# Convolution taps' spectra in four 31-row products on four row groups of PE, in a five-phase audio tower kernel

## The reference

```python
logits = (x @ Wl.T + bl).reshape(B, T, H, K)              # T 125, H 4, K 31
w = softmax(where(valid, logits, -inf), axis=-1)
y = einsum('bthk,btkhd->bthd', w, windows(x)) + bias      # dynamic convolution over time
z = conv1d(y, Wc, 'VALID') + bc                           # Wc (512, 128, 31)
hT = selu(z) @ W2.T + b2
```

## Time and profile before

| what | us |
|---|---|
| median of three executions | 2453.52 |
| lowest, highest | 2449.77, 2454.09 |
| the profiled execution, its own time | 2452.1 |
| its span, first to last instruction | 2450.3 |
| PE busy over the span | 2134.8 (87%) |
| L261, the products of the taps, busy | 134.5, 256 records |

### The profile page before, as it was taken

One profiled execution on the slowest core, in us unless ns is written; L12 is line 12 of the kernel. 1 busy time (PEld: TensorE's weight loads), 2 busy tenths in 40 slices (PEclk: granted clock), 3 DMA queues, 4 the chain that ended last, 5 costly groups with the idle time before them and its releaser, 6 DMA issues. The chain is left out here.

```text
span 2450.3 us, 41718 instructions
## 1 busy us (share of the span) xinstructions
PE 2134.8 (87%) x14183; PEld 1496.8 (61%) x14183; DVE 1588.2 (65%) x3564; ACT 1230.3 (50%) x2063; POOL 915.0 (37%) x763
## 2 busy tenths in 40 slices
PE   5799999979998599999999997999999995776671
PEld 4567868855555466666666664777777774555450
DVE  4432333346777588888888875676767664666673
ACT  2334464344554367677667675555655562332330
POOL 0000000013443378777778772000000001786772
PEclk9999999989999699999999999999999996678995
DMA  7660010019920100000000000000000001214554
GB/s 262 245 245 18 27 34 11 1 43 419 420 117 2 69 1 1 0 0 0 0 0 0 0 1 20 1 0 0 0 0 0 0 1 45 83 43 122 165 154 154
DMA packets 64688, 165.46 MB, mean 68 GB/s; under 512 B 12310, under 2 KB 43460, under 8 KB 55084
## 3 DMA queue, kind: packets, MB, share of 16 engines
q1 hardware_dynamic: 51564, 148.42, 17.0%
q0 software_dynamic: 7104, 12.71, 1.5%
q10 hardware_dynamic: 5888, 2.62, 0.4%
HBM read 68.81 MB, written 96.86 MB: 68 GB/s over the span
## 5 line engine op out<-in xcount | busy, mean ns | idle before, releaser
L1261 POOL TENSOR_TENSOR c_both<-c_hid 128x512 f32<-128x512 f32 x384 | 491.6, 1287 | 144.5 <-ACT c_hid L1234 106.2
L1234 ACT ACTIVATE c_hid<-c_scaled,c_b 128x1024 f32<-128x1024 f32 x384 | 437.1, 1150 | 172.9 <-DVE c_scaled L1308 158.0
L1308 DVE TENSOR_TENSOR c_scaled<-c_p_h,c_shares 128x1024 f32<-128x1024 f32 x384 | 454.5, 1215 | 80.5 <-PE c_p_h L1177 79.5
L1182 PE MATMUL c_p_o<-c_both,c_w 128*128 128x512 f32 x768 | 390.8, 591 | 0.0
L1175 PE MATMUL c_p_h<-c_x_hi,c_w_hi 128*128 128x512 f32 x384 | 291.9, 760 | 2.6 <-DVE c_w_lo L1331 2.6
L624 POOL TENSOR_TENSOR d_ln_rstd<-d_ln_var,d_ln_power 128x2 f32<-128x2 f32 x48 | 33.4, 696 | 525.3 <-DVE d_ln_var L620 525.3
L240 POOL COPY a_work<-a_vec 128x64 f32<-128x64 f32 x4 | 1.2, 303 | 444.4 <-PE a_p_A L322 256.0
L1182 PEld LDWEIGHTS c_p_o<-c_both,c_w 128*128 128x128 f32 x768 | 144.3, 188 | 36.1 <-issue 2.2
L1176 PE MATMUL c_p_h<-c_x_lo,c_w_hi 128*128 128x512 f32 x384 | 152.6, 397 | 0.0
L1492 PEld LDWEIGHTS d_p_s<-d_kk,d_q_bd 128*128 128x128 f32 x768 | 123.9, 192 | 45.9 <-issue 45.9
L1177 PE MATMUL c_p_h<-c_x_hi,c_w_lo 128*128 128x512 f32 x384 | 151.9, 396 | 0.0
(11 more groups left out here) (331 smaller groups left out, 4658.6 us busy)
## 6 DMA issues: line engine op xcount, KB each, us to landing
slots<-b_blank SPq DMA_DIRECT2D x56, 1040.0 KB, 23.7
band_scratch<-a_work SPq DMA_DIRECT2D x16, 1024.0 KB, 5.7
a_work<-band_scratch SPq DMA_DIRECT2D x16, 1023.5 KB, 7.9
e_wb<-e_weights SPq DMA_DIRECT2D x63, 164.0 KB, 2.5
a_raw<-in_Wc SPq DMA_DIRECT2D x16, 512.0 KB, 3.6
e_xb<-slots SPq DMA_DIRECT2D x63, 130.0 KB, 2.2
e_yb<-e_again SPq DMA_DIRECT2D x12, 512.0 KB, 5.6
a_work<-in_x_tok SPq DMA_DIRECT2D x16, 256.0 KB, 8.2
```

What stands on the lines that cost most here:

```text
L1182: nc.tensor.matmul(p_o[s][:, 0:N], w2[:, q, :], both[q % SLOTS][:, :], start=(q == 0), stop=(q == NQ - 1)).then_inc(s_down, 1)
L1234: nc.scalar.activation(hid[q % SLOTS][:, :, :], scaled[q % SLOTS][:, :, :], ACT.Gelu, bias=b1[:, q:q + 1]).then_inc(s_ge, 1)
L1261: nc.gpsimd.tensor_tensor(both[q % SLOTS][:, :], hid[q % SLOTS][:, 0, :], hid[q % SLOTS][:, 1, :], ALU.add).then_inc(s_bo, 1)
L1308: v.tensor_tensor(scaled[q % SLOTS][:, :, :], p_h[q % SLOTS][:, 0:N].unsqueeze(1).to_broadcast([128, 2, N]), shares[s][:, :, :], ALU.mult) ...
```

## The change

`raw` now has 32 rows for a channel slot r (31 taps and an empty one), four slots, so one column block m of raw holds channels 0 + m, 32 + m, 64 + m and 96 + m of a chunk. `dft_k` is the 125-column transform of 31 taps, four times below one another (128 rows, 125 columns). `weights(v)` makes a set: for four m, four products of 31 rows and 125 columns, each on its own row group of PE and into its own bank `p_V[r]`. A set covers 16 channels, four of the old products; there are 32 sets. A bank is copied in one piece (`weights_out(v, r)`), 4 channels x 125, now read at a stride of 125. In the first stage DVE copies all four, two a group; in the turn phases ACT copies r = 0 and 1, DVE r = 2 and 3, one each a group. A set is made in every other (even) group. It waits until all four copies of the set before are done.

The two more banks come from `p_y` and `p_out`, which have one buffer each now, so taps, to_time and project wait for the reader of group k - 1.

```diff
-        dft_k = sb("dft_k", [4 * KT, 4 * NF2])
+        dft_k = sb("dft_k", [128, NF2])
...
-        p_V = [pb("p_V0"), pb("p_V1")]
-        p_y = [pb("p_y0"), pb("p_y1")]
-        p_out1 = pb("p_out1")
-        p_conv, p_out = p_y, [p_log, p_out1]
+        p_V = [pb(f"p_V{r}") for r in range(4)]
+        p_y = pb("p_y")
+        p_conv, p_out = p_y, p_log
...
+        PER, NSET = 4, NO * MPO // 4
+        CHUNK = MPO // PER
+
+        def copied(v):
+
+            late = max(v - CHUNK, 0)
+            return 2 * late, 4 * min(v, CHUNK) + 2 * late
...
-            def weights(m):
-
-                if m % MPC == 0:
-                    i = m // MPC
-                    pe.wait_ge(s_raw[i % WS], 16 * (i // WS + 1))
-                if m >= 2:
-                    pe.wait_ge(s_V, m - 1)
-                nc.tensor.matmul(p_V[m % 2][:, 0:4 * NF2], raw[m // MPC % WS][0:4 * KT, m % MPC, :], dft_k[:, :], start=True,
-                                 stop=True).then_inc(s_vmm, 1)
+            def copied_weights(v):
+                on_act, on_dve = copied(v)
+                if on_act:
+                    pe.wait_ge(s_V[0], on_act)
+                if on_dve:
+                    pe.wait_ge(s_V[1], on_dve)
+
+            def weights(v):
+
+                i = v * PER // MPC
+                pe.wait_ge(s_raw[i % WS], 16 * (i // WS + 1))
+                copied_weights(v)
+                for m in range(PER):
+                    for r in range(4):
+                        rows = slice(32 * r, 32 * r + KT)
+                        last = nc.tensor.matmul(p_V[r][:, m * NF2:(m + 1) * NF2], raw[i % WS][rows, (v * PER + m) % MPC, :],
+                                                dft_k[rows, :], start=True, stop=True, skip_group_check=True)
+                last.then_inc(s_vmm, 1)
...
-                    if g >= 2:
-                        pe.wait_ge(s_R, g - 1)
+                    if g >= 1:
+                        pe.wait_ge(s_R, g)
...
-                if k >= 2:
-                    pe.wait_ge(s_rz, k - 1)
+                if k >= 1:
+                    pe.wait_ge(s_rz, k)
...
-                if k >= 2:
-                    pe.wait_ge(s_h, k - 1)
-                nc.tensor.matmul(p_out[g % 2][:, 0:N], w2[:, o, :], z[g % 2], start=True, stop=True).then_inc(s_omm, 1)
+                if k >= 1:
+                    pe.wait_ge(s_h, k)
+                nc.tensor.matmul(p_out[:, 0:N], w2[:, o, :], z[g % 2], start=True, stop=True).then_inc(s_omm, 1)
...
-                weights(2 * g)
+                if g % 2 == 0:
+                    weights(g // 2)
...
-                weights(2 * g + 1)
...
-                    if o < NO - 1:
-                        weights(MPO * (o + 1) + 2 * g)
+                    if o < NO - 1 and g % 2 == 0:
+                        weights(CHUNK * (o + 1) + g // 2)
...
-            def weights_out(m):
-                dve.wait_ge(s_vmm, m + 1)
-                q = m % MPO
-                v.tensor_copy(V[:, :, 4 * q:4 * q + 4],
-                              p_V[m % 2][:, 0:4 * NF2].rearrange("c (j o) -> c j o", o=4)).then_inc(s_V, 1)
+            def weights_out(v, r):
+                dve.wait_ge(s_vmm, v + 1)
+                if v >= CHUNK and v % CHUNK == 0 and r == 2:
+                    dve.wait_ge(s_zmm, NBK * (v // CHUNK))
+                at = 32 * r + v % CHUNK * PER
+                v_out = V[:, :, at:at + PER]
+                nc.vector.tensor_copy(v_out, p_V[r][:, 0:PER * NF2].rearrange("c (o j) -> c j o", o=PER)).then_inc(s_V[1], 1)
...
-                for g in range(1, NG):
+                for g in range(NG):
+                    if o < NO - 1:
+                        weights_out(CHUNK * (o + 1) + g // 2, 2 + g % 2)
+                    if g == 0:
+                        continue
                     selu(o, g - 1)
```

More of the change, by code:

```diff
@@ L280, in taps @@
                     pe.wait_ge(s_xtok[g % 2], 16 * (g // 2 + 1))
-                    if g >= 2:
-                        pe.wait_ge(s_R, g - 1)
+                    if g >= 1:
+                        pe.wait_ge(s_R, g)
                 for h in range(HK):
-                    last = nc.tensor.matmul(p_y[g % 2][32 * h:32 * h + 32, n * NF2:(n + 1) * NF2],
+                    last = nc.tensor.matmul(p_y[32 * h:32 * h + 32, n * NF2:(n + 1) * NF2],
                                             x_tok[g % 2][0:T, n, 32 * h:32 * h + 32], gt[b % 2][:, h, :],
@@ L328, in to_time @@
                 pe.wait_ge(s_zt, k + 1)
-                if k >= 2:
-                    pe.wait_ge(s_rz, k - 1)
+                if k >= 1:
+                    pe.wait_ge(s_rz, k)
                 for n in range(GB):
-                    last = nc.tensor.matmul(p_conv[g % 2][:, n * SP:(n + 1) * SP], zt[g % 2][:, n, :], idft[:, :],
+                    last = nc.tensor.matmul(p_conv[:, n * SP:(n + 1) * SP], zt[g % 2][:, n, :], idft[:, :],
                                             start=True, stop=True, skip_group_check=True)
@@ L398, in spectrum_out @@
                     act.wait_ge(s_vec, 1)
-                y = p_y[g % 2][:, 0:GB * NF2].rearrange("c (n j) -> c n j", n=GB)
+                y = p_y[:, 0:GB * NF2].rearrange("c (n j) -> c n j", n=GB)
                 parts = y[:, :, 1:NF2].rearrange("c n (f r) -> c f n r", r=2)
@@ L405, in spectrum_out @@
                 nc.scalar.mul(R[:, :, 2 * NB + g * GB:2 * NB + (g + 1) * GB], parts[:, :, :, 0], -1.0).then_inc(s_R, 1)
-            def weights_out(m):
-                act.wait_ge(s_vmm, m + 1)
-                if m % MPO == 0 and m > 0:
-                    act.wait_ge(s_zmm, NBK * (m // MPO))
-                q = m % MPO
-                nc.scalar.copy(V[:, :, 4 * q:4 * q + 4],
-                               p_V[m % 2][:, 0:4 * NF2].rearrange("c (j o) -> c j o", o=4)).then_inc(s_V, 1)
+            def weights_out(v, r):
+                act.wait_ge(s_vmm, v + 1)
+                if v % CHUNK == 0 and r == 0:
+                    act.wait_ge(s_zmm, NBK * (v // CHUNK))
+                at = 32 * r + v % CHUNK * PER
+                nc.scalar.copy(V[:, :, at:at + PER],
+                               p_V[r][:, 0:PER * NF2].rearrange("c (o j) -> c j o", o=PER)).then_inc(s_V[0], 1)
             def z_out(o, i):
@@ L434, in exp_z @@
                     act.wait_ge(s_z, k - 1)
-                nc.scalar.activation(ez[g % 2], p_conv[g % 2][:, 0:N].rearrange("o (n s) -> o n s", n=GB), ACT.Exp,
+                nc.scalar.activation(ez[g % 2], p_conv[:, 0:N].rearrange("o (n s) -> o n s", n=GB), ACT.Exp,
                                      bias=ln_alpha[:, :]).then_inc(s_ez, 1)
@@ L514, in selu @@
                 dve.wait_ge(s_ez, k + 1)
-                v.tensor_scalar(rz[g % 2], p_conv[g % 2][:, 0:N].rearrange("o (n s) -> o n s", n=GB), -SELU_ALPHA,
+                v.tensor_scalar(rz[g % 2], p_conv[:, 0:N].rearrange("o (n s) -> o n s", n=GB), -SELU_ALPHA,
                                 -SELU_ALPHA, ALU.add, ALU.max).then_inc(s_rz, 1)
@@ L526, in add_h @@
                 at = hT[:, g * GB:(g + 1) * GB, :]
-                src = p_out[g % 2][:, 0:N].rearrange("p (n s) -> p n s", n=GB)
+                src = p_out[:, 0:N].rearrange("p (n s) -> p n s", n=GB)
                 if o == 0:
@@ L540, in _ @@
             for g in range(NG):
-                weights_out(2 * g)
+                for r in (0, 1) if g % 2 == 0 else (2, 3):
+                    weights_out(g // 2, r)
                 if g + AHEAD < NG:
                     shifted(g + AHEAD)
-                weights_out(2 * g + 1)
                 if g + AHEAD < NG:
@@ L2572, in layouts @@
     d["dft_t"] = f(waves.astype(np.float32))
-    four = np.zeros((4, KT, NF2, 4))
-    for i in range(4):
-        four[i, :, :, i] = waves[0:KT]
-    d["dft_k"] = f(four.reshape(4 * KT, 4 * NF2).astype(np.float32))
+    four = np.zeros((4, 32, NF2))
+    four[:, 0:KT] = waves[0:KT]
+    d["dft_k"] = f(four.reshape(128, NF2).astype(np.float32))
     back = waves[0:SP].T * (2.0 / T)
```

25 lines of the change are left out of this document (10 added, 15 removed).

## The result

| | before | after |
|---|---|---|
| median, us | 2453.31 | 2427.41 |
| lowest, highest | 2449.77, 2454.09 | 2424.3, 2429.41 |
| profiled execution, its span | 2452.1, 2450.3 | 2426.93, 2425.1 |
| PE busy over the span | 2134.8 | 2096.5 |
| products of the taps, busy | 134.5, 256 records | 38.4, 1024 records |

The changed kernel takes 0.9896 of the time of the kernel before, interval 0.9881 to 0.9911, four executions each: 26 us less. The forecast was 2412, 41 us less, in a range of 2397 to 2430. Direction and mechanism were right and the wide range held; the gain was three fifths of what was worked out, and 2427 lies outside the range that the prediction gave its own forecast (2402 to 2424).

What follows compares the result with a forecast made beforehand. PE bounds the turn phases and the first stage's tail, the x_tok load loop its middle. 2452.1 - 39.2 (chunks 0 to 2) + 4.2 (last chunk) - 5.4 (first stage) = 2411.7, forecast 2412 us, range 2397 to 2430.

Steps and rivals of the forecast that it cites:

- rival 2: Chunks 0 to 2: strided V copies take twice as long and DVE becomes the bound, about 2426 us; chance 0.10.
- the set: 16 matmuls on four row groups: 8 x 0.11 + 0.28 = 1.16 us, bounds 0.88 and 3.8.
- the pair: Turn phases: an odd and an even group take 5.64 us; wrong if less than 5.3 or more than 6.0.
- the stretch up to the eleventh group: First stage up to the 11th group's taps: wrong if it moves by more than 8 us.
- rivals 1: Row groups overlap only two at a time, a set takes 2.1 us, about 2438 us; chance 0.07.
- rival 3: Passes run one by one, a set costs 3.8 us, slower than before at about 2482 us; chance 0.05.
- The loop through one p_conv: Turn phases: to_time of the next group waits until relu has read p_conv, 2.28 us a group without a set.
- PE's own road: Turn phases, one to_time to the next through project and turn: 2.20 us, 3.36 with a set.
- Rival 4: One-buffer waits are less than worked out, a pair comes near 5.06 us, about 2397 us; chance 0.10.
- The last chunk: Turn phase without V products only loses: 14 x (2.28 - 2.035) = 3.4, and 0.77 at its last to_time, +4.2 us.
- The middle: DMA-bound part of the first stage: V products stand in PE's slack, gain 0; lower clock +3 us, bounds 0 and 12.
- The tail: PE-bound last groups of the first stage: eleven V products go, two sets come, waits add 0.8; -6.6 us.

Runs made afterwards that it cites:

- one-row-group run: The changed kernel with all four products of a column block reading rows 0 to 30, so on one row group: 2546.91 us.
- filled run: The changed kernel with the second sequence's spread products repeated once or twice in groups 2 to 10 of the first stage: 2427.85 us, ratio 0.9886.
- wide-load run: The changed kernel with dft_k loaded at its old width, 128 rows of 500 columns, only 125 columns read: 2430.42 us, ratio 0.9903.

## Why the prediction was right, and by how much it was off

**The range held partly by luck.** Of the head's 4.5 us the prediction had 0.5. The other 4 are above all the rows of one load and the scatter of the start, which nothing in it foresaw; without them the profiled execution would have taken 2431 us, above the 2430 that closed the range. That upper end was there for rival 2, which did not come. Of the signs named, the set (1.30 us, bound 1.6), the pair (5.96, bound 6.0) and the stretch up to the eleventh group stayed within their bounds, the pair barely.

**What bounds the kernel.** Right. PE was the limit of the turn phases, and there the gain was made: 33.0 us in chunks 0 to 2, of which 26 are left.

**The set.** Forecast 1.16 us from L755 and L765, 8 x 0.11 and 0.28 for the edges, measured 1.30: the edges came to 0.42. The bounds were 0.88 and 3.8; the overlap of the row groups, which no row had shown for 128 weight columns, is full. Taking the value from the nearest rows was right; rivals 1 and 3 fall, and the one-row-group run shows rival 3's price to be real.

**The loop through one p_conv.** The mis-sized term that matters most. Forecast 1.06 + 0.62 + 0.56 + 0.04 = 2.28, measured 1.14 (1.17 behind a set) + 0.61 + 0.56 + 0.15 = 2.46 (2.49). The first term was read in the kernel before, where to_time never waited and its first weights were loaded under other work: the first load starts 0.42 us ahead of to_time there (242.25 to 242.67), and 0.03 ahead behind a wait (225.78 to 225.81). The 0.04 for a release, bounded by 0 to 0.1, was an estimate without a row, and 0.15 lies outside its bounds. Together 0.18 to 0.21 us a group, in 21 odd groups and the 14 of the last chunk. PE's own road was also short, 1.12 + 0.72 + 0.53 = 2.37 for 2.20, for the same reason and for the edge. A pair took 5.96 for 5.64: 2.1 us a chunk, which is the difference between -39.2 and -33.0. Rival 4, that the waits would be less than worked out, was wrong in its sign.

**The last chunk.** Forecast +4.2, measured +8.2. 14 x (2.46 - 2.035) = 6.0 instead of 3.4; from the first to the last to_time it is +6.8 for +4.2. Behind the last to_time come +1.4 that the prediction had at nothing: the last project waits for add_h of the group before, 0.6 us, and then runs at the lower clock (PE):

```profile
490.13 1.62 PE L357 MATMUL a_p_log<-a_work,a_w 128*128 128x384 f32 x2 [1.57 <-DVE hT L545]
```

It takes 1.62 us instead of 0.88. The lower clock at this place shows in two of the six traces with one buffer here; the other four have 0.88, and their phase takes 47.2 to 47.3 us.

**The first stage.** Forecast -5.4, measured -2.9 (-4.5 up to the first spread, +1.6 behind it).
- Up to the first spread: forecast -0.5, measured -4.5, of which 2.2 are scatter and some 1.6 the rows of the load, which the prediction did not have.
- From there to the second logits: forecast -1.3, measured +0.7. The first set takes 2.02 us for 0.97 and the spread behind it 1.89 for 1.27; the wait for ACT's copy takes up one of the V products that went, and spectrum_out costs 0.31 as worked out.
- The middle: gain 0 was right, and clock +3 within 0 to 12 had the right mechanism. It came to +5.6 us, of which 4.2 are logits and taps at the lower clock: five of the nine logits products were at it for the most part, none before. Their place behind the wait makes them part of the loop. I argued from the mean clock of the stretch, 0.95, but what counts is the clock in the 2 us behind the wait. That a busier PE would undo this is argued, not shown; the filled run gave back 0.9 of the 4.2.
- The tail: forecast -6.6, measured -4.7 (46.1 to 41.4 us). Waits for spectrum_out came as worked out (0.9 us in sum). Not seen was that the removed V product also covered ACT's copy L403, for which PE now waits 1.6 us in three places there (0.5 before), and a set is 1.10, not 0.97.

**Product phases and later ones.** Product phases were called unchanged; three of them grew by 0.25 us each, as one buffer alone makes them. That of chunk 0 takes 28.85 us in seven traces and 30.5 in five, on both sides of the change: in the wide-load run the granted clock of its first 7.3 us was 0.77, in the changed kernel 1.00. The later phases took 1.8 us more. In the four kernels with the old V products they took 1926.9 to 1928.2, in the changed kernel and the seven built on it 1928.4 to 1932.5; this small step stays unexplained.

**Copies at a stride.** Priced at nothing, and they cost nothing.

## What to carry to other kernels

When a step of a loop turns from covered to waited for, don't take its length from a trace in which it was covered: add the weight load and the release that a wait exposes, here 0.2 us a group. Where a product has few rows, row groups with a bank each are worth it even at the price of double buffers, and the buffers can be given back in the phase where the banks are free. And taking work off an engine in a stretch that a load bounds brings nothing there, and can cost clock; look instead for the order that holds the load back.

## What the runs showed of the hardware that was not expected

- 16 fp32 products of 31 rows by 125 columns, each on its row group with its own weights of 128 columns, take 1.10 us as a block; on one row group 3.76 us. A block that goes from full array to row groups and back pays 0.09 and 0.11 us at its edges, so half a block costs 0.65 and not 0.55.
- With those passes on one row group the granted clock was 0.82 over a turn phase in which PE was busy 98% of the time, and single blocks ran at the 1.2 GHz level (0.227 us a pass, 0.118 at the other). In the first such fall, at about 244 us, PE had just run a set at full clock, 3.83 us long, and had last stood idle for 0.70 us ahead of 239.17. On four row groups the same passes had 1.00.
- A 242 KB load of 124 rows held back the load behind it by 2.6 us more than a 250 KB load of 128 rows; 1.6 us of that reached the first spread.
- A product that starts behind a wait for another engine takes about 0.08 us longer to its reader's start, and starts 0.15 us after that engine's end.
